# Two weight loads split by rows over two issuing engines, in a fused LoRA and expert layer on one core

## What is computed

```python
base_out = einsum('bti,oi->bto', x, W) + b            # first layer
lora_h   = einsum('bti,bir->btr', x, lora_As[slot])   # slot: one per sequence, rank 16
y        = base_out + einsum('btr,bro->bto', lora_h, lora_Bs[slot]) * 2.0

base_out = einsum('bsi,oi->bso', y, base_w) + base_b  # second layer
hidden   = einsum('bsi,ri->bsr', y, A)                # 64 columns
probs    = softmax(einsum('bsi,ei->bse', y, router_w))  # 16 experts, the two largest kept, normalised
delta    = einsum('bse,bsr,eor->bso', combine, hidden, B)
out      = x + base_out + delta * 0.5
```

## Time and profile before

| | us |
|---|---|
| median of 3 runs (lowest to highest) | 101.38 (101.21 to 102.25) |
| the profiled execution, its own time | 101.33 |
| its span, first to last instruction | 99.5 |
| TensorE busy | 95.6 (96%) |
| VectorE busy | 66.6 (67%) |
| ScalarE busy | 41.5 (42%) |
| GpSimd busy | 22.2 (22%) |

### The profile page before, as it was taken

One profiled execution on the slowest core, in us unless ns is written; L12 is line 12 of the kernel. 1 busy time (PEld: TensorE's weight loads), 2 busy tenths in 40 slices (PEclk: granted clock), 3 DMA queues, 4 the chain that ended last, 5 costly groups with the idle time before them and its releaser, 6 DMA issues.

```text
span 99.5 us, 1810 instructions
## 1 busy us (share of the span) xinstructions
PE 95.6 (96%) x572; PEld 87.0 (87%) x572; DVE 66.6 (67%) x184; ACT 41.5 (42%) x101; POOL 22.2 (22%) x34
## 2 busy tenths in 40 slices
PE   6799999999999999999999999999999999999990
PEld 6699999999999999998898799888787877878980
DVE  5669996997485885899977567257949275572101
ACT  3514636968787546756522610451334022040000
POOL 4100004224999965108123000000000000000000
PEclk9999999999999999999999999999999999999999
DMA  1999659999558675891780836516228074020211
GB/s 42 331 326 410 207 123 361 267 361 352 150 91 205 203 239 151 232 231 37 221 253 25 214 119 163 153 43 184 106 76 255 26 194 122 0 105 0 105 59 53
DMA packets 8379, 16.91 MB, mean 170 GB/s; under 512 B 1507, under 2 KB 4067, under 8 KB 8370
## 3 DMA queue, kind: packets, MB, share of 16 engines
q1 hardware_dynamic: 7762, 16.41, 55.1%
q10 hardware_dynamic: 576, 0.39, 1.2%
q0 software_dynamic: 32, 0.00, 0.0%
HBM read 13.28 MB, written 2.16 MB: 155 GB/s over the span
## 4 chain that ended last, share of the span: by engine, by line
PE 93%; DMA 3%; DVE 0%; ACT 0%; issue 0%
PE pair L820 90%; DMA w_raw_all<-w_cat 3%; PE pair L965 1%; PE pair L967 1%; PE pair L985 1%; DVE xn L814 0%; ACT w_hi_all L420 0%; PE pair L955 0%; PE pair L944 0%; PE pair L942 0%; PE pair L934 0%
## 5 line engine op out<-in xcount | busy, mean ns | idle before, releaser
L820 PE MATMUL pair<-e_hi,w_hi_all 128*128 128x512 f32 (+1 forms) x72 | 27.1, 376 | 0.0
L820 PE MATMUL pair<-e_hi,w_lo_all 128*128 128x512 f32 (+1 forms) x72 | 26.7, 370 | 0.0
L820 PE MATMUL pair<-e_lo,w_hi_all 128*128 128x512 f32 (+1 forms) x72 | 26.7, 370 | 0.0
L533 ACT ACTIVATE w_hi_all<-exp_raw_all 128x512 fp32r<-128x512 f32 x16 | 9.7, 630 | 15.3 <-DVE exp_raw_all L755 15.3
L820 PEld LDWEIGHTS pair<-e_hi,w_lo_all 128*128 128x128 f32 x72 | 13.6, 188 | 2.5
L820 PEld LDWEIGHTS pair<-e_hi,w_hi_all 128*128 128x128 f32 x72 | 13.6, 188 | 2.5
L820 PEld LDWEIGHTS pair<-e_lo,w_hi_all 128*128 128x128 f32 x72 | 13.6, 189 | 2.0
L762 DVE TENSOR_TENSOR w_lo_all<-exp_raw_all,w_hi_all 128x512 fp32r<-128x512 f32 x16 | 10.4, 689 | 4.5 <-ACT w_hi_all L533 4.0
L755 DVE TENSOR_TENSOR exp_raw_all<-w_raw_all 128x512 f32<-128x512 f32 x16 | 11.2, 741 | 0.1
L769 DVE TENSOR_TENSOR xn<-pair,xn 128x512 f32<-128x512 f32 x7 | 4.8, 690 | 8.9 <-PE pair L820 8.9
L820 PE MATMUL pair<-p_hi,x_hi 128*128 128x304 f32 x32 | 10.0, 311 | 0.0
(11 more groups left out here) (107 smaller groups left out, 162.2 us busy)
## 6 DMA issues: line engine op xcount, KB each, us to landing
w_raw_all<-spill SPq DMA_DIRECT2D x16, 256.0 KB, 4.2
xt_raw<-x_t SPq DMA_DIRECT2D x4, 512.0 KB, 6.3
exp_raw_all<-experts SPq DMA_DIRECT2D x4, 512.0 KB, 8.7
xn<-x_n SPq DMA_DIRECT2D x4, 512.0 KB, 5.8
out<-xn SPq DMA_DIRECT2D x7, 256.0 KB, 2.8
w_raw_all<-w_cat SPq DMA_DIRECT2D x2, 552.0 KB, 6.4
c_stack<-c_hi SPq DMA_DIRECT2D x7, 74.0 KB, 3.9
c_stack<-c_lo SPq DMA_DIRECT2D x7, 74.0 KB, 4.2
```

The source lines that it names most:

```text
L533: nc.scalar.activation(gt_hi[:, t % 2, js, :], g[:, js, :], ACT.Copy).then_inc(gh_done, 1)
L820: return nc.tensor.matmul(out_ap, lhs, rhs, start=first, stop=last)
```

## The change

TensorE's first half of block 0 is now m = 2, 3, which read W's right half. `W_RIGHT` and `W2_LEFT` of block 0 are neighbours and are loaded as one run of columns, `LEAD` (256 to 807, 2208 bytes a row, 276 KB). SP loads its rows 0 to 63 and ScalarE its rows 64 to 127, with one semaphore `in_lead` that both raise; VectorE and ScalarE wait for 32 on it. SP goes on with `W2_RIGHT` and ScalarE with the left half of W (`W_REST`). Block 1 is loaded whole, rows 0 to 63 by SP and 64 to 127 by ScalarE, with 32 on `in_w[1]`; `in_w_next` is gone. Ahead of its third issue ScalarE copies one column of zeros to `spare`, and with this first activation the table load stands in front of that issue. The remaining loads and conversions keep their order.

```diff
--- before.py
+++ after.py
@@ -54,7 +54,10 @@
 FOLDS = (1, 0, 2, 3)
 
 W_LEFT, W_RIGHT = slice(0, D // 2), slice(D // 2, D)
+
+W_LEAD, W_REST = W_RIGHT, W_LEFT
 W2_LEFT, W2_RIGHT = slice(D, D + W2H), slice(D + W2H, D + W2N)
+LEAD = slice(W_LEAD.start, W2_LEFT.stop)
 WARM_UP = 13
 
 ACT_TABLES = 2
@@ -106,6 +109,7 @@
         x_hi = sb("x_hi", [P, 2, KC, P], F32R)
         x_lo = sb("x_lo", [P, 2, KC, P], F32R)
         ident = sb("ident", [P, P])
+        spare = sb("spare", [P, 1])
         ones = sb("ones", [P, P], F32R)
 
         idle = nc.const_aps.tensor(0.0, (P, 2 * P), F32).bitcast(F32R)
@@ -175,9 +179,9 @@
 
 
         in_w = [None] + [sem(f"in_w{k}") for k in range(1, KC)]
-        in_w_side = [sem("in_w_left"), sem("in_w_right")]
-        in_w2_side = [sem("in_w2_left"), sem("in_w2_right")]
-        in_w_next = sem("in_w_next")
+        in_lead = sem("in_lead")
+        in_rest = sem("in_rest")
+        in_w2_right = sem("in_w2_right")
         in_slots = sem("in_slots")
         in_lora = sem("in_lora")
         in_b = sem("in_b")
@@ -192,7 +196,7 @@
         stored = sem("stored")
 
         wh_first = sem("wh_first")
-        wh_left = sem("wh_left")
+        wh_lead = sem("wh_lead")
         wh_next = sem("wh_next")
         wh_done = sem("wh_done")
         wl_first = sem("wl_first")
@@ -261,11 +265,10 @@
                 sp.dma_start(w_raw[:, k, :], w_cat[k]).then_inc(in_w[k], 16)
 
 
-            for n, cols in enumerate((W2_LEFT, W2_RIGHT)):
-                sp.dma_start(w_raw[:, 0, cols], w_cat[0, :, cols]).then_inc(in_w2_side[n], 16)
-
-            sp.dma_start(w_raw[:, 1, D // 2:], w_cat[1, :, D // 2:]).then_inc(in_w[1], 16)
-            sp.dma_start(w_raw[:, 1, W_LEFT], w_cat[1, :, W_LEFT]).then_inc(in_w_next, 16)
+            sp.dma_start(w_raw[0:P // 2, 0, LEAD], w_cat[0, 0:P // 2, LEAD]).then_inc(in_lead, 16)
+            sp.dma_start(w_raw[:, 0, W2_RIGHT], w_cat[0, :, W2_RIGHT]).then_inc(in_w2_right, 16)
+
+            sp.dma_start(w_raw[0:P // 2, 1, :], w_cat[1, 0:P // 2, :]).then_inc(in_w[1], 16)
             for k in range(2, KC):
                 load_w(k)
             sp.dma_start(xt_raw[:, 0:2, :], x_t[:, 0:2, :]).then_inc(in_xt[0], 16)
@@ -413,20 +416,24 @@
 
         @block.scalar
         def _(act):
-            for n, cols in enumerate((W_LEFT, W_RIGHT)):
-                act.dma_start(w_raw[:, 0, cols], w_cat[0, :, cols]).then_inc(in_w_side[n], 16)
-            act.wait_ge(in_w_side[0], 16)
-            for cols in (slice(0, P), slice(P, 2 * P)):
-                nc.scalar.activation(w_hi[:, 0, cols], w_raw[:, 0, cols], ACT.Copy).then_inc(wh_left, 1)
-            act.wait_ge(in_w_side[1], 16)
-            nc.scalar.activation(w_hi[:, 0, W_RIGHT], w_raw[:, 0, W_RIGHT], ACT.Copy).then_inc(wh_done, 1)
+
+            act.dma_start(w_raw[P // 2:, 0, LEAD], w_cat[0, P // 2:, LEAD]).then_inc(in_lead, 16)
+            act.dma_start(w_raw[:, 0, W_REST], w_cat[0, :, W_REST]).then_inc(in_rest, 16)
+
+            nc.scalar.activation(spare[:, :], nc.const_aps.tensor(0.0, (P, 1), F32), ACT.Copy)
+            act.dma_start(w_raw[P // 2:, 1, :], w_cat[1, P // 2:, :]).then_inc(in_w[1], 16)
+            act.wait_ge(in_lead, 32)
+            for cols in (slice(2 * P, 3 * P), slice(3 * P, 4 * P)):
+                nc.scalar.activation(w_hi[:, 0, cols], w_raw[:, 0, cols], ACT.Copy).then_inc(wh_lead, 1)
+            act.wait_ge(in_rest, 16)
+            nc.scalar.activation(w_hi[:, 0, W_REST], w_raw[:, 0, W_REST], ACT.Copy).then_inc(wh_done, 1)
             act.wait_ge(in_slots, 16)
             for t in range(NT - ACT_TABLES, NT):
                 slot = act.value_load(slot_row[0:1, t:t + 1], min_val=0, max_val=SLOTS - 1)
                 src = tables[bass.ds(slot, 1), :, :].rearrange("o p n -> p (o n)")
                 act.dma_start(lora_raw[:, t, :], src).then_inc(in_lora, 16)
-            for cols, loaded, done in ((W_RIGHT, in_w[1], wh_next), (W_LEFT, in_w_next, wh_done)):
-                act.wait_ge(loaded, 16)
+            act.wait_ge(in_w[1], 32)
+            for cols, done in ((W_RIGHT, wh_next), (W_LEFT, wh_done)):
                 nc.scalar.activation(w_hi[:, 1, cols], w_raw[:, 1, cols], ACT.Copy).then_inc(done, 1)
             for k in range(2, KC):
                 act.wait_ge(in_w[k], 16)
@@ -597,7 +604,10 @@
             nc.vector.memset(low_row[F_BIAS:F_BIAS + 1, :], 0.0).then_inc(first_set, 1)
 
             def first_block_hi(n, cols):
-                dve.wait_ge(in_w2_side[n], 16)
+                if n == 0:
+                    dve.wait_ge(in_lead, 32)
+                else:
+                    dve.wait_ge(in_w2_right, 16)
                 nc.vector.tensor_copy(w_hi[:, 0, cols], w_raw[:, 0, cols]).then_inc(wh_first, 1)
 
             def first_block_lo(cols, done):
@@ -607,15 +617,15 @@
             first_block_hi(0, W2_LEFT)
             dve.wait_ge(wh_first, 1)
             first_block_lo(W2_LEFT, wl_first)
-            dve.wait_ge(wh_left, 2)
-            first_block_lo(W_LEFT, wl_done)
+            dve.wait_ge(wh_lead, 2)
+            first_block_lo(W_LEAD, wl_done)
             first_block_hi(1, W2_RIGHT)
             dve.wait_ge(wh_first, 2)
             first_block_lo(W2_RIGHT, wl_first)
             dve.wait_ge(wh_done, 1)
-            first_block_lo(W_RIGHT, wl_done)
+            first_block_lo(W_REST, wl_done)
             for k in range(1, KC):
-                dve.wait_ge(in_w[k], 16)
+                dve.wait_ge(in_w[k], 32 if k == 1 else 16)
                 nc.vector.tensor_copy(w_hi[:, k, D:], w_raw[:, k, D:]).then_inc(wh_first, 1)
                 dve.wait_ge(wh_first, k + 2)
                 nc.vector.tensor_tensor(w_lo[:, k, D:], w_raw[:, k, D:], w_hi[:, k, D:].bitcast(F32),
@@ -836,12 +846,13 @@
                 mm(pairs[m][:, out_cols], lhs[:, 0, m * P:(m + 1) * P], rhs[:, 0, cols], first, False)
 
             sides = ((slice(BANK - W2H, BANK), W2_LEFT), (slice(BANK, BANK + W2H), W2_RIGHT))
-            for half, rows_done in enumerate((wh_left, wh_done)):
-                ms = range(half * KC // 2, (half + 1) * KC // 2)
+            for half, rows_done in enumerate((wh_lead, wh_done)):
+
+                ms = range((1 - half) * KC // 2, (2 - half) * KC // 2)
                 for side, (out_cols, cols) in enumerate(sides):
                     pe.wait_ge(wh_first, side + 1)
-                    for m in ms:
-                        pe.wait_ge(rows_done, 1 if half else m + 1)
+                    for n, m in enumerate(ms):
+                        pe.wait_ge(rows_done, 1 if half else n + 1)
                         fold_quarter(m, w_hi, w_hi, out_cols, cols, True)
                     pe.wait_ge(wl_first, side + 1)
                     for m in ms:
```

## The result

| | before | after |
|---|---|---|
| median, us (lowest to highest, 6 runs each) | 101.35 (101.21 to 102.25) | 104.06 (102.95 to 105.18) |
| ratio of the times, 95% interval | 1 | 1.0199 (1.0153 to 1.0246) |
| the profiled execution, us | 101.33 | 103.46 |
| its span, us | 99.5 | 101.7 |

The change makes the kernel 2% slower; the forecast of no change was wrong, and its range of 100.9 to 102.5 missed. Ratios and intervals leave disturbed runs out and medians don't, so a ratio need not be that of the two medians.

A forecast was written before the change was run, and what follows sets the result against it. TensorE was taken to bound the kernel, its fold start set by the opening transfer. Opening +0.04, all other terms nothing: span 99.54, plus 1.83 gives 101.37, forecast 101.4, no change, range 100.9 to 102.5.

The forecast's parts named there:

- The frame: Whole run: after 4.37 us only TensorE waits move the end; each microsecond of fold start is one of the run.
- Opening piece: First weight load: lands between 3.65 and 3.97, taken as 3.77 against VectorE's start at 3.73, so +0.04 us.
- sign of being wrong: Opening load: a landing at 4.4 was listed among the observations that would show the forecast wrong.
- The late bound: Opening load: 64-row loads run at 320 instead of 360 GB/s, costing 0.07 us, so landing by 3.97.
- The other bound: Opening load: half as many, longer pieces could gain some 0.25 us, landing at 3.65.
- The rest of block one: Remaining first-block weights, W2_RIGHT and the rest of W: still in time for their conversions, costing nothing.
- Second block: Second weight block: both halves in by 7.13, TensorE may start at 7.72 and needs it at 7.99; cost nothing, cover 0.27.
- Issue and table load: ScalarE's added copy and issue end long before 3.77, no time; SP issues blocks three and four 0.45 earlier.
- The late half behind the table load: Rival: ScalarE's second-block half issued late behind the table load; 104.2 (chance 0.12) or 102.5 (chance 0.04).
- The gain of 0.25: Rival: opening gains all of 0.25 and lands at 3.65, at most 0.23 of the run; 101.1 to 101.25, chance 0.15.
- Halves serialize: Rival: opening and second-block halves move at 180 GB/s, +0.54 and +1.57; time 103.2, chance 0.04.

The follow-up runs named there:

- c2: The kernel after, unchanged, run once more beside later runs on one chip: 104.01 us, ratio 1.0252.
- c4: The kernel after with the opening's halves swapped, SP loading rows 64 to 127 and ScalarE rows 0 to 63: 104.06 us, ratio 1.0264.
- b4: The kernel after with the opening as one 128-row load by SP and the second block whole on SP: 102.27 us, ratio 1.0047.
- c1: The kernel after with both 64-row opening halves on SP and the second block whole on SP: 103.55 us, ratio 1.019.
- a2: The kernel before with 10 warm-up matmuls instead of 13, transfers untouched: 103.12 us, ratio 1.0128.
- a4: The kernel after with the second block loaded whole by SP, the opening left split by rows: 104.35 us, ratio 1.0111.
- c3: a4 with 17 warm-up matmuls instead of 13 and the left half of W issued by SP before the second block: 102.3 us, ratio 1.0075.
- a1: The kernel after with 18 warm-up matmuls instead of 13: 103.71 us, ratio 1.0103.
- a3: The kernel after with the opening split by columns again, 128 rows each on SP and ScalarE: 102.06 us, ratio 0.9978.
- b1: a3 with the second block split by columns over both queues instead of by rows: 102.32 us, ratio 1.0045.
- b2: a3 with both 64-row halves of the second block issued by SP: 101.97 us, ratio 0.999.
- b3: a3 with the second block loaded whole by SP: 102.0 us, ratio 1.0026.

## Why the prediction was wrong, point by point

**The frame held.** A microsecond by which the fold starts later is a microsecond of the run, nothing behind the second block moves the end: the last column above. What failed is the work done inside the frame, in four places.

**"Opening piece", +0.04 with bounds 3.65 and 3.97: the step that failed.** VectorE started at 4.69, 4.38 (c2) and 4.41 (c4): +0.65 to +0.96, outside both bounds, and where the prediction had set its sign of being wrong (4.4). The late bound was made from a rate: the spread loads of 64 rows ran at 320 GB/s in the middle of their transfer, so 194 KB should lose 0.07. This transfer was not paid by the rate in its middle. It was paid from the issue to the last step of the semaphore, and there the two ends grew: the issue takes 0.57 for 0.40 (b4), the first packet comes at 2.09 for 1.78 on SP's queue and at 2.63 for 2.02 on ScalarE's, and the last step of the semaphore stands 1.13 behind the last packet (0.42 in b4). The middle, which the bound was made from, cost little: the last row is through 0.16 behind b4's. The price of the issue stood in the very group that was used: two issues of 64 rows in 1.09, 0.545 each, against 0.43 for 128 rows. It was read for its rate and not for its length.

The other bound went astray too: half of a gain of 0.25 from longer and fewer pieces was taken in. b4 has the long rows, and VectorE starts at 3.83, no earlier than before. Nor is half a load half the work: b4 lands 276 KB in 3.1 us, c1's second half 138 KB in 3.5.

**A step that was missing: what the longer pause does to TensorE.** The prediction moved the fold's start and kept its pace. In the profile after, 1.38 of the 2.15 us is pace: 14 passes at about twice the spacing. a2 shows such slow passes on unchanged transfers: three warm-up matmuls less, a pause of 0.77 for 0.55, and half of the passes are slow in its trace, at 1.3% over ten runs. No row of the kernel before shows a slow fold pass; but its warm-up stands at the lower pace and the fold at the upper, so the trace did say that TensorE rises about when the fold starts, and the sum should have asked what more idle time in front does to that. The table gives the trend and its limits: the late rises stand behind pauses of 0.77 to 1.41 (a2, c2, after, c1), but a4 and c4 were at the upper pace after 0.70 and 0.97, and c3 rose only at 6.0 without any. With the same 13 warm-up matmuls the clock records begin anywhere from 3.62 (before) to 10.32 (c1). That the longer pause makes a late rise likelier is argued from these traces, not shown. The Trainium skill, page "TensorE: Matmul & The Clock Gate", section "What's actually happening", says that the same kernel can show different numbers of slow matmuls from one run to the next; the two executions of the kernel after agree, with 14 slow passes in the first trace and 12 in c2.

**"The rest of block one: nothing."** The second half of W was converted at 6.59 in place of 4.55; at 7.48 in a1, where TensorE paid 1.10 for it, and at 8.51 in a4, where it paid 2.17. It is as large as before, but its issue starts at 1.38 behind a 64-row one and takes 0.83, and it lands 5.2 us later. That it kept its size was no reason that it would keep its time. (A slip without weight: VectorE's low part of it was before the sixth conversion from 3.73 on, not the fifth, as the piece at 4.08 that the earlier trace rows leaves out is two.)

**"Second block: nothing, cover 0.27."** It landed at 8.9 in place of 7.13, 1.5 past the cover. Whether that is paid depends on the run: nothing in the first trace, where TensorE was later still, 0.48 in a1, 0.68 in c2, 1.10 in c4. With the opening by columns its form made no difference beyond half a per cent (a3, b1, b2, b3), though the traced executions of a3, b1 and b3 stood 0.92, 1.74 and 0.51 in front of it.

**"Issue and table load: no time"** was right for the table load and wrong for the issues: the third one started at 2.30 and not at 1.7. It did not wait for the table load, which was running; the two issues in front of it had taken 0.58 and 0.83. And SP's next two blocks were issued at 2.51, 0.10 earlier than before (2.61) and not 0.45.

**The rivals.** The late half behind the table load (0.16 in all) did not happen: that its 104.2 is the number nearest to the measured 104.06 is luck. The gain of 0.25 did not happen either. *Halves serialize*, at 0.04 and 103.2, came nearest in kind, and its warning was the one to heed: the Trainium skill, page "SBUF — State Buffer", section "Can I just issue two DMAs to hit both halves?", advises one transfer over all 128 rows, and b4 against the kernel after (3.83 against 4.69 and 4.38) agrees with the advice. The mechanism as priced there, 180 GB/s throughout, is not what the trace shows: from 2.6 to 3.0 us the packet records hold 62 opening rows, 342 GB/s, from both queues. The prediction had set the rule aside on two mid-run transfers that nobody waits for at their first byte.

**How the causes cover each other.** Late opening, slow passes, late left half of W and late second block stand one behind the other, and TensorE pays only those that stick out. So in a1 the slow passes were gone and the second block started 0.29 later still, while a3, which removed the first cause, removed all. c3 takes out most of what follows and keeps the late opening: 0.85 of c2's 2.56 us are left, so about two thirds of the loss are what follows the late opening, and one third is the lateness. The split is rough, as c3's opening is itself 0.18 earlier than c2's (4.20 for 4.38).

**Open.** Why a 64-row load takes longer to issue, and why so much time lies between its last packet and the last step of the semaphore; which of the two halves lands last; why TensorE rose at 8.0 in c2 and by 4.9 in c4 after a like pause; whether rows or queues slow the second block. No version that ran is faster than the kernel before: a3 at 0.998 and b2 at 0.999 are no different from it.

## What to carry to other kernels

Price a transfer that opens a kernel by its issue and its time to landing, not by the rate of its middle alone: splitting it by partition rows over two engines here halved the bytes of each load, and the whole was there 0.65 to 0.96 us later. Where a first matmul moves, ask what the longer idle time does to TensorE's pace, and lengthen the warm-up with it before judging. Where two loads raise one semaphore, read from the packets which of them is late, not from the landings. Where several late things stand behind one another, undoing the second or third shows nothing until the first is gone.

## What the runs showed of the hardware

- A first load on SP takes 0.56 to 0.57 us to issue over 64 rows (138 KB in after, c1, c2), 0.40 over 128 rows (148 KB in a3, 276 KB in b4). There the rows matter and the bytes don't. It is not the whole rule: in the kernel after SP's second issue, over 128 rows, took 0.56 too, and its third, 64 rows of the second block, 0.49 (0.56 and 0.59 for such halves in b2).
- Of two 64-row halves issued within 0.02 us of each other, ScalarE's first packet comes 0.40 to 0.54 us behind SP's and its last ends 0.35 to 0.57 behind, in six traces (after, a1, a4, c2 to c4), and with the rows swapped as well. With 128 rows on each queue the first packets are 0.24 apart (2.02 and 1.78 in the kernel before).
- The last step of the semaphore stands 0.81 to 1.13 us behind the last packet of a 64-row opening (those six and c1), 0.42 in b4.
- The Trainium skill, page "DMA: Bandwidth & Descriptors", section "Issuing engines are not separate DMA queues", says that issuing from several engines saves only the time of the issue. Here the two issues did run side by side, and the opening was still later than in one load from one engine (b4).
- A DMA issue on ScalarE runs beside its table load (2.30 within 2.24 to 3.52).
- TensorE's slow passes stand 0.247 us apart for 296 columns, which is 1.2 GHz, while the granted clock in the answer by windows reads 1.00. The spacing of the matmuls is the safer reading; the clock records in the packed traces, where they hold the rise, agree with it (8.06 in c2).
